# Expert tiles of two 128-row halves, each half with an expert of its own, in a transformer block on one core

## The reference

```python
def _L0_ffn_ref(x, gate_w, dense_1_w, dense_1_b, dense_2_w, dense_2_b):
    # B*L = 8192 tokens, D = 256, E = 8 experts, F = 512, TOP_K = 2
    xf = x.reshape(B * L, D)
    gate = xf @ gate_w
    weights, sel = jax.lax.top_k(gate, k=TOP_K)
    weights = jax.nn.softmax(weights, axis=-1)
    h = jnp.einsum('ecd,td->tec', dense_1_w, xf) + dense_1_b[None]
    h = swiglu(h)          # g, v = even, odd columns, clipped at 9
    y = jnp.einsum('edf,tef->ted', dense_2_w, h) + dense_2_b[None]
    y_sel = jnp.take_along_axis(y, sel[:, :, None], axis=1)
    out = jnp.einsum('tkd,tk->td', y_sel, weights)
    return out.reshape(B, L, D)
...
x = x + gb * _L0_ffn_ref(h, ...)
```

## Time and profile before

| what | value |
|---|---|
| median of 3 runs | 2089.19 us (2083.57 to 2095.52) |
| the profiled execution | 2092.97 us |
| its span, first to last instruction | 2091.0 us |
| granted clock of the matrix engine, mean | 0.946 of full speed |
| share of the span, PE, PEld, DVE, ACT, POOL | 90%, 73%, 67%, 46%, 48% |
| stretch from the first expert matmul to the end | 1454.38 to 2091 us |

### The profile page before, as it was taken

How to read it: one execution, slowest core, us unless ns; L and a number is a source line. 1 busy time by engine, 2 the same in 40 slices (tenths; PEclk the granted TensorE clock), 3 DMA queues, 4 the chain that set the end, 5 groups by cost and what they waited for, 6 DMA issues and landing times. The chain is left out here.

```text
span 2091.0 us, 57683 instructions
## 1 busy us (share of the span) xinstructions
PE 1881.6 (90%) x19628; PEld 1521.4 (73%) x19629; DVE 1407.0 (67%) x3577; ACT 964.4 (46%) x1734; POOL 1011.3 (48%) x1131
## 2 busy tenths in 40 slices
PE   4999999999999999979888988931999999999997
PEld 2788888888888888746655665621888888888886
DVE  6657776676677766559888888861656666666665
ACT  3333333333334343346454455511655556666564
POOL 4222222222222222235777777753566666666664
PEclk8989999999999999989999988965999999999999
DMA  4222212212222221235334334412455555554444
GB/s 149 64 57 56 55 55 55 55 55 55 55 55 55 55 55 40 46 113 160 97 123 146 110 120 134 125 48 71 70 92 92 91 92 93 91 91 91 91 91 56
DMA packets 155520, 172.90 MB, mean 83 GB/s; under 512 B 35140, under 2 KB 136199, under 8 KB 155328
## 3 DMA queue, kind: packets, MB, share of 16 engines
q1 hardware_dynamic: 101248, 96.90, 17.7%
q0 software_dynamic: 36352, 56.78, 14.6%
q10 hardware_dynamic: 17856, 18.37, 2.5%
HBM read 109.40 MB, written 53.99 MB: 78 GB/s over the span
## 5 line engine op out<-in xcount | busy, mean ns | idle before, releaser
L1905 POOL DMA_INDIRECT out<-experts_y,experts_entry x144 | 237.2, 1647 | 193.5 <-DVE experts_y L1881 166.3
L678 PE MATMUL mixer_pv<-w_V,mixer_prob 128*128 128x33 f32 x2048 | 256.2, 281 | 0.0
L678 PEld LDWEIGHTS mixer_pv<-w_V,mixer_prob 128*128 128x128 f32 x2048 | 243.5, 195 | 12.1 <-issue 1.0
L1846 DVE TENSOR_SCALAR experts_v<-experts_v 128x512 f32<-128x512 f32 x144 | 74.3, 516 | 220.2 <-ACT experts_v L1820 212.5
L811 ACT ACTIVATE mixer_prob<-mixer_sc 128x1024 f32<-128x1024 f32 x128 | 131.2, 1025 | 174.6 <-PE mixer_sc L668 174.6
L1820 ACT ACTIVATE experts_g<-experts_pg,x_b 128x256 f32<-128x256 f32 x288 | 120.9, 471 | 181.4 <-PE experts_pv L131 181.3
L1895 POOL DMA_INDIRECT experts_rows<-scratch_xs,experts_entry x144 | 168.4, 1169 | 59.2 <-issue 43.0
L915 DVE TENSOR_REDUCE w_mx<-mixer_sc 128x8 bf16<-128x1024 f32 x128 | 156.1, 1219 | 46.9 <-PE mixer_sc L642 46.4
L1035 POOL TENSOR_TENSOR mixer_x<-mixer_mix,mixer_hres 128x256 f32<-128x256 f32 x64 | 46.5, 726 | 290.5 <-DVE mixer_mix L887 289.6
L129 PE MATMUL experts_pg<-experts_xT,x_w 128*128 128x256 f16 x576 | 158.1, 275 | 11.8 <-issue 7.7
L1520 POOL DMA_INDIRECT scratch_queue<-mlp_entry,mlp_slot x128 | 141.3, 1104 | 51.2 <-issue 38.4
(11 more groups left out here) (364 smaller groups left out, 5661.0 us busy)
## 6 DMA issues: line engine op xcount, KB each, us to landing
mixer_x<-in_x SPq DMA_DIRECT2D x16, 512.0 KB, 10.7
w_Kz<-mixer_Kt SPq DMA_DIRECT2D x64, 128.0 KB, 2.8
mixer_hres<-mixer_h SPq DMA_DIRECT2D x16, 512.0 KB, 3.0
scratch_xs<-scratch_mod SPq DMA_DIRECT2D x16, 512.0 KB, 10.5
scratch_x<-mixer_x SPq DMA_DIRECT2D x16, 512.0 KB, 3.1
mlp_xa<-scratch_x SPq DMA_DIRECT2D x16, 512.0 KB, 4.3
mlp_stage<-in_x_w SPq DMA_DIRECT2D x16, 512.0 KB, 4.3
mlp_xb<-scratch_x SPq DMA_DIRECT2D x16, 512.0 KB
```

What stands on the lines that cost most here:

```text
L678: last = pe.matmul(pvO[:, i, :], prob[:, n % 2, at:at + P], V[:, n, i, :], start=True, stop=True)
L1846: dve.tensor_scalar(v[:, q, :], v[:, q, :], -8.0, 10.0, ALU.max, ALU.min).then_inc(v_cut.sem, 1)
L1905: pool.indirect_dma_start(out=out, out_offset=bass.IndirectOffsetOnAxis(ap=entry[:, s, t, 0:1].bitcast(I32), axis=0), in_=y[:, s % 2, t, : ...
```

## The change

Where a tile was 256 rows of one expert, it is now two halves of 128 rows, and each half has its own expert and its own first row. `plan` counts in parts of 128 rows and fills 136 columns in place of 72; there are 128 full parts plus 7 for the rounding, which makes 68 tiles in place of 72. The loop runs as before in sixes; the tiles left over stand outside it.

In `experts`, each engine reads two expert numbers for a tile (`experts_of`). `up` makes its products for one half at a time, so 96 matmuls of 128 columns in place of 48 of 256. ACT does the biased functions in 16 instructions of 128x128 in place of 8 of 128x256. DVE adds the second bias in two instructions in place of one. SP loads the entries in two DMAs, each with a row number of its own. In the scatter, the second half waits until the DMA of the first has landed, since both halves may now hold the same token.

```diff
-def plan(nc, keep, capacity, n_tiles):
+def plan(nc, keep, capacity, n_parts):
...
-                lambda: dve.tensor_scalar(cnti[:], cnt[:], float(ROWS - 1), None, ALU.add),
-                lambda: dve.tensor_scalar(cnti[:], cnti[:], ROWS.bit_length() - 1, None, ALU.logical_shift_right),
+                lambda: dve.tensor_scalar(cnti[:], cnt[:], float(P - 1), None, ALU.add),
+                lambda: dve.tensor_scalar(cnti[:], cnti[:], P.bit_length() - 1, None, ALU.logical_shift_right),
...
-            with eng.Fori(1, groups - 1) as i:
+            with eng.Fori(1, whole) as i:
...
-        def expert_of(eng, tile):
-            return eng.value_load(keep["tiles"][0:1, 0, bass.ds(tile, 1)], min_val=0, max_val=E - 1)
+        def experts_of(eng, tile):
+            return [eng.value_load(keep["tiles"][0:1, 0, bass.ds(tile * RT + t, 1)], min_val=0, max_val=E - 1)
+                    for t in range(RT)]
...
-                sp.dma_start(entry[:, s, :, :], scratch["queue"][bass.ds(r, ROWS), :].rearrange(
-                    "(t p) d -> p t d", p=P)).then_inc(entry_in[s].sem, 16)
+                for t in range(RT):
+                    sp.dma_start(entry[:, s, t, :], scratch["queue"][bass.ds(r[t], P), :]
+                                 ).then_inc(entry_in[s].sem, 16)
...
-                            for k in range(KD):
-                                last = hi_lo_products(
-                                    pe, bank[:, q, f * ROWS:(f + 1) * ROWS],
-                                    [a[:, bass.ds(e * KD + k, 1), col:col + P].rearrange("p a n -> p (a n)")
-                                     for a in x["w1"]],
-                                    [xT[:, u, i, k, :] for i in range(2)], k == 0, k == KD - 1)
+                            for t in range(RT):
+                                at = f * ROWS + t * P
+                                for k in range(KD):
+                                    last = hi_lo_products(
+                                        pe, bank[:, q, at:at + P],
+                                        [a[:, bass.ds(e[t] * KD + k, 1), col:col + P].rearrange("p a n -> p (a n)")
+                                         for a in x["w1"]],
+                                        [xT[:, u, i, k, t * P:(t + 1) * P] for i in range(2)], k == 0, k == KD - 1)
...
-                            [a[:, bass.ds(e * 2 + f // 2, 1), f % 2, :].rearrange("p a n -> p (a n)") for a in x["w2"]],
+                            [a[:, bass.ds(e[t] * 2 + f // 2, 1), f % 2, :].rearrange("p a n -> p (a n)") for a in x["w2"]],
...
-                            act.activation(dst[:, q, f * ROWS:(f + 1) * ROWS], bank[:, q, f * ROWS:(f + 1) * ROWS], fn,
-                                           bias=x["b1"][:, bass.ds(e, 1), bias + 2 * q + f]).then_inc(done.sem, 1)
+                            for t in range(RT):
+                                at = f * ROWS + t * P
+                                act.activation(dst[:, q, at:at + P], bank[:, q, at:at + P], fn,
+                                               bias=x["b1"][:, bass.ds(e[t], 1), bias + 2 * q + f]
+                                               ).then_inc(done.sem, 1)
...
-            def scatter(tile, i, s):
-                before = slot_after(i, s, -1)
-                wait_alone(pool, added[before[1]].sem, added[before[1]].at(before[0] + 1, 0), passed)
-                wait_alone(pool, y_gated.sem, y_gated.at(tile, RT), passed)
-                for t in range(RT):
-                    pool.indirect_dma_start(
...
+            def scatter(tile, i, s, t):
+                if t == 0:
+                    before = slot_after(i, s, -1)
+                    wait_alone(pool, added[before[1]].sem, added[before[1]].at(before[0] + 1, 0), passed)
+                else:
+                    wait_alone(pool, added[s].sem, added[s].at(i, 16 * t), passed)
+                wait_alone(pool, y_gated.sem, y_gated.at(tile, t + 1), passed)
+                pool.indirect_dma_start(
...
-    n = 2 * NB * L // ROWS + E - 1
-    return n + -n % 6
+    parts = 2 * NB * L // P + E - 1
+    return -(-parts * P // ROWS)
```

More of the change, by code:

```diff
@@ L1566, in plan @@
         cnti = m.sb("cnti", [P, E], I32)
-        tile, ex, before, first = (row(n, n_tiles) for n in ("tile", "ex", "before", "first"))
-        ge = m.sb("ge", [1, n_tiles, E])
-        gn = m.sb("gn", [1, n_tiles, E])
+        tile, ex, before, first = (row(n, n_parts) for n in ("tile", "ex", "before", "first"))
+        ge = m.sb("ge", [1, n_parts, E])
+        gn = m.sb("gn", [1, n_parts, E])
         start = m.sb("start", [P, E])
@@ L1674, in experts @@
     last_row = E * capacity
-    groups = n_tiles // SLOTS
-    assert n_tiles % SLOTS == 0 and groups > 2
+    whole = (n_tiles - LEAD - 1) // SLOTS
+    assert whole > 1
     with ExitStack() as ctx:
@@ L1691, in experts @@
         py = m.ps("py", [P, 2, 512])
[L1692 removed]
+        entry_in = [m.counter(f"entry_in{s}", 16 * RT) for s in range(SLOTS)]
         row_in = [m.counter(f"row_in{s}", 16 * RT) for s in range(SLOTS)]
@@ L1709, in loop @@
                 body(s, 0, s)
-            with eng.Fori(1, groups - 1) as i:
+            with eng.Fori(1, whole) as i:
                 for s in range(SLOTS):
                     body(i * SLOTS + s, i, s)
-            for s in range(SLOTS):
-                body((groups - 1) * SLOTS + s, groups - 1, s)
+            for tile in range(whole * SLOTS, n_tiles):
+                body(tile, tile // SLOTS, tile % SLOTS)
         def left(tile, ahead):
@@ L1790, in body @@
                 first = isinstance(tile, int) and tile == 0
-                e_up = expert_of(pe, tile)
-                e_down = None if first else expert_of(pe, tile - 1)
+                e_up = experts_of(pe, tile)
+                e_down = None if first else experts_of(pe, tile - 1)
                 up(tile, s % 2, e_up)
@@ L1913, in body @@
                 if not (isinstance(tile, int) and tile == 0):
-                    scatter(tile - 1, *slot_after(i, s, -1))
+                    for t in range(RT):
+                        scatter(tile - 1, *slot_after(i, s, -1), t)
             for s in range(LEAD):
@@ L1918, in _ @@
             loop(pool, body)
-            scatter(n_tiles - 1, groups - 1, SLOTS - 1)
+            for t in range(RT):
+                scatter(n_tiles - 1, *divmod(n_tiles - 1, SLOTS), t)
             for s in range(SLOTS):
-                pool.wait_ge(added[s].sem, added[s].at(groups, 0))
+                pool.wait_ge(added[s].sem, added[s].at(len(range(s, n_tiles, SLOTS)), 0))
 def n_tiles(NB):
-    n = 2 * NB * L // ROWS + E - 1
-    return n + -n % 6
+    parts = 2 * NB * L // P + E - 1
+    return -(-parts * P // ROWS)
 def program(nc, din, out, scratch, NB):
```

52 lines of the change are left out of this document (26 added, 26 removed).

## The result

| | before | after |
|---|---|---|
| median | 2092.04 us (2083.57 to 2095.52, 4 runs) | 2450.49 us (2447.66 to 2453.66, 4 runs) |
| ratio, with its 95% interval | | 1.1721 (1.1678 to 1.1763) |
| the profiled execution, span | 2091.0 us | 2446.4 us |
| granted clock, mean | 0.946 | 0.918 |

The changed kernel is 17% slower: 358 us. The forecast was 2413 us, 321 us above the before-median of this comparison. So the time lies inside the stated range of 2350 to 2480 us; the direction and nine tenths of the size were there, and 37 us were not.

The account below looks back on a forecast made before the run. PE bounds the kernel before; its instruction queue would bound the changed one at a summed 13.8 us a tile: 68 x 13.8 = 938 us for 621 us, plus 6 us once, +323 us, forecast 2413 us, range 2350 to 2480.

Parts of the forecast that it names:

- What bounds the kernel now: Experts' stretch: PE's own time sets the 8.62 us tile; its instruction queue, 8.15 us, lies just under, idling PE 0.21 us.
- The array's price of 128-column products: PE's array in `up`: 96 x 0.056 = 5.4 us against 48 x 0.109 = 5.2 us, costing 0.15 us.
- The groups of `up`: PE's queue: 32 groups of three products with register work per tile, 0.247 us each, 7.9 us.
- The reads: PE's queue: four expert numbers per tile in place of two, 0.67 us each, 2.7 us, no longer covered.
- The transposes' issue: PE's queue handing out eight transposes per tile with their wait: between 8 x 0.027 and 8 x 0.109 us, taken as 0.5 us.
- The end of the loop: PE's queue: branch of 0.21 us and its registers once in six tiles, 0.1 us a tile.
- Once only: Outside the tiles: `plan`'s wider instructions, the last tile's second scatter wait (2.9 us) and first entries' DMAs, together 6 us.
- The rival of the clock: PE's idling lowers the granted clock: 16.8 us a tile if it stays low, 2616 us, chance 0.04; short drops hidden.
- The rival of the scatter's wait: POOL's 9.65 us a tile bounds while PE's queue keeps up: +41 us, 2130 us; chance 0.04.
- Only the issue of products: PE's 0.247 us groups hold, but reads and part of the waits are hidden: 11.2 us a tile, 2236 us; chance 0.07.
- That the change does what it says: PE's queue keeps the array's pace and hides the reads: 8.8 us a tile, 2072 us, faster; chance 0.03.
- The signs that were named: In the experts' stretch: `up` matmuls about 0.08 us apart, tile 13 to 14.5 us, PE busy no more than 75%, among others.

## Why the prediction was right, and where it was not

**What bounds the kernel now** held. The idle of 0.21 us with the releaser "issue" was the queue. The kernel with one read per tile less showed it by taking it away.

**The array's price of 128-column products** (0.15 us a tile) held. Without register work `up` took 5.3 us where it took 5.1 us before. With one expert the ordinary tile rose by 0.4 us, part of it a longer wait for the queue before the first product. The 0.082 us that the prediction drew from the earlier trace rows is the queue's pace and not the array's: without registers 128-column products start 0.056 us apart.

**The groups of `up`** (0.247 us each, 32 of them) held at 0.255 us. It was shown to be register work and not the pace of the products: half the groups without registers left the tile at 8.9 us.

**The reads** (2.7 us for four) measured 2.7 us, and two reads less gave 77 us where 79 were expected.

**`down`** (2.0 + 0.2 us) measured 2.2 us.

**The transposes' issue** (0.5 us, the middle of two bounds) measured 0.2 us. The lower bound was the right one: the products without registers passed the queue nearly free in the kernel of 128 columns too. The same error, 0.055 us per product without registers, stood in the sum for the kernel before, so its 8.15 us was too high. That the kernel before was nonetheless touched by its queue has another reason, the short lead: the queue was some 18 products ahead at most where I read it, and a read takes 0.67 us in one piece. For the changed kernel this made no difference, for the kernel with four reads it made 9.9 us out of 9.5.

**The end of the loop** is the term that was mis-sized: "The branch of 0.21 us and its registers once in six tiles: 0.1 us." It was taken at the length of the old body. The new one is 2149 entries in place of 1290, and the jump took 4.15 us. A tile with a jump stood 4.6 us over its neighbours, of which 0.6 us was in the sum, and eight times 4.0 us is 32 of the 37 us. The other 58 distances between tiles sum to 795 us, which is 58 times 13.7 us, the sum without its term for the loop. That this is so exact is luck in part: the ordinary tiles of the loop took 13.9 us, those outside of it 13.3 us and the first one 9.7 us. The prediction had counted what the added entries cost the queue and had not asked whether the body still fits where the jump expects it.

**Once only**: the end was charged with one added landing, 2.9 us. POOL's last four scatters show three, as the last tile is ready before the one ahead of it has landed:

```profile
2432.81 1.55 POOL L1915 DMA_INDIRECT out<-experts_y,experts_entry  x1 [3.10 <-DMA out<-experts_y,experts_entry]
2437.38 1.55 POOL L1915 DMA_INDIRECT out<-experts_y,experts_entry  x1 [3.02 <-DMA out<-experts_y,experts_entry]
2442.10 1.55 POOL L1915 DMA_INDIRECT out<-experts_y,experts_entry  x1 [3.17 <-DMA out<-experts_y,experts_entry]
```

One of these three stood before as well, so two are new, some 3 us more than the sum had. 32 and 3 us leave 2 us, which is less than the runs tell apart.

**The rival of the clock** did what the prediction said of short drops. Two stretches of four tiles each, in the same view as the earlier trace rows, differ in the granted clock and not in the pace; the transposes shown are those of the first stretch:

```profile
1547.50:1603.00 55.50, 46.66 (x513) 40.38 (x514) 20.93 (x40) 25.56 (x76) 21.80 (x16) 0.88 0.32 59
2246.50:2302.00 55.50, 46.15 (x515) 35.31 (x513) 20.77 (x41) 25.74 (x78) 20.33 (x16) 1.00 0.29 49
```

```profile
L1759 PE MATMUL experts_pt<-w_identh,experts_rows x32: 219/219/219, 1558.7 to 1600.6; 128*128 128x128 f16 x32
```

At 0.88 the tiles came every (41.9 - 0.4) / 3 = 13.8 us, at 1.00 every 13.9 us. The clock fell to 0.50, the level of 1.2 GHz, for 3.4 us a time in most of these drops, and the array made them up against a slower queue. What makes it fall stays open: PE stood still for some 2.3 us before every tile, and from 2239.0 to 2399.5 us it stayed at 1.00 all the same.

**The rival of the scatter's wait** had the right mechanism and the right size, 9.65 us a tile against 9.7 and 9.9 us measured, and the wrong place: it comes second. **Only the issue of products** (11.2 us a tile) needed reads under cover, which they are not. **That the change does what it says** would have needed a free queue and a free landing, and the run without registers shows that the second alone forbids it.

**The signs that were named** came, but for two. PE was busy 46.15 of 55.5 us in the second stretch above, 83% and not 75% or less: its rows overlap, as the prediction feared. And the products of `up` don't start 0.08 us apart but three at 0.06 us and then a pause, as shown below; 0.08 us is only their mean.

## What to carry to other kernels

Read the instruction queue of the busiest engine like an engine: add up its register instructions, reads of values and waits per round, and compare with the engine's own time; "issue" before the first product of a round, however short, says that the two are close. A change that halves the size of products with addresses from registers doubles their register work, though the arithmetic stays, and four rounds of work saved (34 us) stood against 68 times 5.3 us. Keep a value read once in its register for the next round, and watch a loop body's length, as past some size each jump back costs microseconds.

## What the runs showed of the hardware

- On PE's queue a group with two register instructions took 0.247 to 0.255 us, about 0.12 us each by an estimate, and weight loads and matmuls with addresses at hand next to nothing: 96 more entries per tile's `up` changed 3.9 us to 4.2 us.
- PE's queue was at most some 18 products ahead of the array in the tiles that were read. With 256-column products, four reads and a wait of 3.0 us together left the array idle for some 1.6 us, and two reads of 1.4 us for 0.2 us.
- A jump back took 0.21 us with bodies of 1290 and 1583 entries on PE and 3.4 to 4.5 us with bodies of 1866, 2117, 2149 and 2575. Programs written out in full, without any jump, ran at full pace, up to an array busy for 99.6%.
- 128-column products with a weight load each ran at 0.06 us apart, as in these rows of the changed kernel's timeline of PE, between the pauses of its queue:

```profile
1610.27 0.23 PE L129 MATMUL experts_pv<-experts_xT,x_w 128*128 128x128 f16 x1
1610.33 0.22 PE L130 MATMUL experts_pv<-experts_xT,x_w 128*128 128x128 f16 x1
1610.39 0.22 PE L131 MATMUL experts_pv<-experts_xT,x_w 128*128 128x128 f16 x1
1610.51 0.23 PE L129 MATMUL experts_pv<-experts_xT,x_w 128*128 128x128 f16 x1
```

The three products of a group start 0.06 us apart, and the next group 0.24 us after the first.

What stays open: what exactly decides the length at which a jump becomes long, and whether it is counted in entries or in bytes, as no lengths but these were tried; and what makes the granted clock fall behind some pauses of PE and not behind others.
